# First stage of a language-model tower: each four gathers wait for the four issued three groups ago

## The reference

```
emb = word_emb[x] + pos_emb                        # 64 x 128 x 192
for each of 3 graphs: ev = word_emb[ids]           # 64 x 128 x 192
    g_j = relu(mean_over_rows(adj_j @ ev) @ W_j.T + b_j)     # 64 x 16
y  = concat([emb, g_1, g_2, g_3]) @ W_proj.T + b_proj
h  = layernorm(y) * gamma + beta                   # first stage up to here
h += long_convolution(layernorm(h)) + bias term    # filter from a small sine network
h += mixture_of_experts(layernorm(h))              # 8 experts, top 2, 192 -> 768 -> 192, gelu
```

## Time and profile before

| | us |
|---|---|
| median of 3 runs | 1004.51 (1003.2 to 1005.33) |
| profiled execution | 999.54 |
| its span | 997.7 |
| PE busy | 872.5 (87%) |
| DVE busy | 658.9 (66%) |
| POOL busy | 636.2 (64%) |
| ACT busy | 535.8 (54%) |

### The profile page before, as it was taken

How to read it: one execution, slowest core, us unless ns; L and a number is a source line. 1 busy time by engine, 2 the same in 40 slices (tenths; PEclk the granted TensorE clock), 3 DMA queues, 4 the chain that set the end, 5 groups by cost and what they waited for, 6 DMA issues and landing times.

```text
span 997.7 us, 22836 instructions
## 1 busy us (share of the span) xinstructions
PE 872.5 (87%) x7469; PEld 828.4 (83%) x7469; DVE 658.9 (66%) x2142; ACT 535.8 (54%) x1271; POOL 636.2 (64%) x552
## 2 busy tenths in 40 slices
PE   3969899898788839894779999999999999999993
PEld 2959899888788828893569999999999989999993
DVE  3167857777667664977846777677666666666662
ACT  1222232223222134579947777777777767777771
POOL 6777777777777500100057887588777768888886
PEclk9957556655665659997589999999999999999997
DMA  7427647457374339882956445835754554343454
GB/s 252 124 83 254 202 123 252 140 189 246 89 245 143 123 84 286 211 254 65 216 154 173 60 60 99 247 57 93 193 127 62 96 132 61 62 64 62 60 58 45
DMA packets 99788, 138.31 MB, mean 139 GB/s; under 512 B 13427, under 2 KB 81430, under 8 KB 97654
## 3 DMA queue, kind: packets, MB, share of 16 engines
q0 software_dynamic: 39552, 53.26, 27.8%
q1 hardware_dynamic: 59142, 73.59, 23.9%
q10 hardware_dynamic: 1008, 10.34, 2.8%
HBM read 98.14 MB, written 39.02 MB: 137 GB/s over the span
## 4 chain that ended last, share of the span: by engine, by line
POOL 26%; PE 26%; DMA 25%; issue 12%; DVE 6%; ACT 3%; DVEq 1%; POOLq 0%; SPq 0%
DMA out<-Hs,id_s 20%; POOL ev_g L520 16%; POOL emb_g L512 6%; POOL blob L536 3%; PE bank L798 3%; PE bank L800 3%; PE bank L799 3%; DMA emb_g<-in_word_emb,ids_i 2%; PE bank L779 2%; PE bank L780 2%; PE bank L782 2%; PE bank L781 2%; PE bank L783 2%; DVE hstats L1156 2%; DMA ev_g<-in_word_emb,ids_i 1%
## 5 line engine op out<-in xcount | busy, mean ns | idle before, releaser
L974 ACT ACTIVATE Hs<-bank,U 128x256 bf16<-128x256 f32 x426 | 214.1, 502 | 120.9 <-PE bank L783 120.9
L550 POOL DMA_INDIRECT out<-Hs,id_s x142 | 234.1, 1648 | 65.9 <-issue 46.8
L520 POOL DMA_INDIRECT ev_g<-in_word_emb,ids_i x192 | 188.3, 981 | 67.6 <-issue 56.4
L536 POOL DMA_INDIRECT blob<-xtab_d,id_g x142 | 144.9, 1020 | 122.6 <-DVEq L1339 79.7
L975 ACT ACTIVATE Hs<-bank,U 128x256 f32<-128x256 f32 x426 | 216.5, 508 | 0.0
L1361 DVE TENSOR_TENSOR Hs<-Hs 128x512 bf16<-128x512 f32 x213 | 147.2, 692 | 103.0 <-ACT Hs L975 102.6
L798 PE MATMUL bank<-U,Hs 128*128 128x192 bf16 x852 | 210.1, 247 | 0.3 <-issue 0.3
L800 PE MATMUL bank<-U,Hs 128*128 128x192 bf16 x852 | 208.8, 245 | 0.0
L799 PE MATMUL bank<-U,Hs 128*128 128x192 bf16 x852 | 208.5, 245 | 0.0
L779 PE MATMUL bank<-wst,U 128*128 128x256 bf16 x426 | 116.7, 274 | 1.3 <-DVE wst L1350 1.3
L780 PE MATMUL bank<-wst,U 128*128 128x256 bf16 x426 | 116.7, 274 | 0.0
(11 more groups left out here) (216 smaller groups left out, 1651.3 us busy)
## 6 DMA issues: line engine op xcount, KB each, us to landing
adj_s<-in_adj SPq DMA_DIRECT2D x48, 256.0 KB, 8.0
ev_g<-kpad_d SPq DMA_DIRECT2D x24, 512.0 KB, 5.8
U<-blob_d SPq DMA_DIRECT2D x14, 771.0 KB, 4.7
wst<-in_wsrc SPq DMA_DIRECT2D x8, 1344.0 KB
blob_d<-blob ACTq DMA_DIRECT2D x7, 1443.0 KB, 5.5
U<-blob_d SPq DMA_DIRECT2D x14, 672.0 KB, 5.5
xtab_d<-U SPq DMA_DIRECT2D x4, 1552.0 KB, 16.2
out<-Hs SPq DMA_DIRECT2D x4, 1536.0 KB, 12.8
```

The lines of the kernel that those rows point to most:

```text
L520: pool.indirect_dma_start(ev_g[:, p, j, b, :], None, t["word_emb"], bass.IndirectOffsetOnAxis(ap=ids_i[:, 1 + j, i * Q + b:i * Q + b + 1], ...
L536: pool.indirect_dma_start(xg_f[:, q % RX, h, :], None, xtab_d, bass.IndirectOffsetOnAxis(ap=id_g[:, 2 * q + h:2 * q + h + 1], axis=0)).the ...
L550: pool.indirect_dma_start(out, bass.IndirectOffsetOnAxis(ap=id_s[:, 2 * q + h:2 * q + h + 1], axis=0), yo[:, q % RY, h, :], None, compute_ ...
L974: f(hh[w][:, d, :], ps, ACT.Gelu, bias=bi[:, d:d + 1])
```

## The change

Every group of four gathers now waits for the landing of the group issued three groups before it. Before, E, v1 and v2 waited for the group two before them, and v0 had no landing wait. The waits on `emb_t` and `gvec` and the gathers themselves stay.

```diff
--- before.py
+++ after.py
@@ -506,16 +506,17 @@
             def gathers(i):
                 p = i % 2
                 if i > 0:
-                    pool.wait_ge(ev_in[1 - p][1], 16 * Q * ((i - 1) // 2 + 1))
+                    pool.wait_ge(ev_in[1 - p][0], 16 * Q * ((i - 1) // 2 + 1))
                 after(pool, emb_t, i - 1)
                 for b in range(Q):
                     pool.indirect_dma_start(emb_g[:, p, b, :], None, t["word_emb"],
                                             bass.IndirectOffsetOnAxis(ap=ids_i[:, 0, i * Q + b:i * Q + b + 1], axis=0)).then_inc(emb_in[p], 16)
                 after(pool, gvec, i - 1)
                 for j in range(GRAPHS):
-                    landed = emb_in[p] if j < 2 else ev_in[p][0]
-                    if j > 0:
-                        pool.wait_ge(landed, 16 * Q * (i // 2 + 1))
+                    if j == 2:
+                        pool.wait_ge(emb_in[p], 16 * Q * (i // 2 + 1))
+                    elif i > 0:
+                        pool.wait_ge(ev_in[1 - p][j + 1], 16 * Q * ((i - 1) // 2 + 1))
                     for b in range(Q):
                         pool.indirect_dma_start(ev_g[:, p, j, b, :], None, t["word_emb"],
                                                 bass.IndirectOffsetOnAxis(ap=ids_i[:, 1 + j, i * Q + b:i * Q + b + 1], axis=0)).then_inc(ev_in[p][j], 16)
```

## The result

| | before | after |
|---|---|---|
| median of the runs | 1005.33 us (5 runs, 1003.2 to 1008.03) | 997.75 us (5 runs, 995.12 to 998.45) |
| ratio, 95% interval | | 0.9926 (0.9898 to 0.9954) |
| profiled execution, its span | 999.54, 997.7 | 997.75, 995.9 |

The changed kernel is 7.6 us faster. A second comparison on another occasion gave 0.9901 (0.9873 to 0.9928), which is 9.9 us of 999.88; its medians, 988.43 against 999.88 us, lie 11.4 apart. So the change is worth 7 to 10 us by the two ratios, 5 to 13 by their intervals; 10.5 had been forecast.

A forecast was written before the change was run, and what follows sets the result against it. POOL's 11.4 us of pauses and PE's 11.2 us of gather waits were taken to bound the first stage side by side; 11.2 less 0.7 for delayed loads gives 10.5, so 1004.5 becomes 994.0 us, range 990.5 to 1001.

The forecast's parts named there:

- the added wait: On POOL, one more wait instruction per turn, condition already true: cost 0, at most 0.8 us.
- the buffers: POOL's wait for PE to have used buffers of two turns ago: 7.6 us left at turn 4, cost 0.
- PE held its pace: PE, turns 10 to 14: without gather waits they take 98.6 us, 19.72 a turn, as turns 6 to 9 did.
- The pauses: POOL, first stage: all seven waits for landings go, 11.4 us gained on POOL, bounds 0 and 11.4.
- the long gathers: POOL gathers that take longer while DVE splits an expert's weights; the change was said not to touch them.
- What then ends last: End of first stage: POOL's last landing 332.8, PE 333.1, so PE sets the end and the stage gains 11.2 us.
- The burst: Expert store, expert load and adjacency loads together: extra gathers delay direct loads, priced 0.7 us, up to 4.9.
- rival B: Late loads delay DVE's adjacency sums and PE waits at L602, halving the gain: 998.2 us; chance 0.19.
- C: POOL's deeper queue fills as well and it pauses one group later: no gain, 1004.5 us; chance 0.09.
- D: TensorE gets its lower clock more often without pauses: slower, 1011 us; chance 0.07 with any other loss.
- The spans: Whole profiled execution: span 997.7 less 10.5 gives 987.2 us; the same gain on the median gives 994.0.

The follow-up runs named there:

- the first pair: First profiles of the kernel before and the changed kernel; medians 1005.33 and 997.75 us, ratio 0.9926.
- the repetition: Kernel before and changed kernel each run once more, programs unchanged; 999.36 us (1.0007) and 988.43 us (0.9901 to before).
- short loads: Only 128 of 2688 columns loaded for experts 1 to 7, in the kernel before (995.40 us, 0.9924) and the changed kernel (992.73 us, 0.9918).

## Why the prediction was right, and where it was off

Right: the direction, the cause and the place. The seven pauses went, no new wait came in their place at POOL, landings stayed under 11.25 us, the added wait cost nothing that shows (gap 0.30 as before), the buffers stayed free (5.5 us at turn 4, the closest place, of the 7.6 before), PE held its pace (turns 10 to 14 took 98.9 us with no wait for a gather, 98.6 forecast), and what the stage gained came through to the experts' first fetch (7.9 and 9.7 us in the two pairs). 997.75 us lies in the range; the gain was 7.6 (9.9 on the second occasion), not 10.5. In the first pair the distance from 10.5 comes from two errors of the same sign, told next.

*The pauses*, priced at 11.4 us, are the mis-sized term. The waits view counts the whole idle time ahead of the gather, and 7 x 0.30 of it is the issue gap that stays. The removable part was 9.2 us (8.7 in the repetition).

*A term that was missing.* "The change does not touch those", said of the long gathers, holds for their cause and not for their length. Which gather meets DVE's subtraction or an adjacency sum, and where in it, shifts with POOL's pace: 251.6 to 256.6 us of gathers with the same passes on DVE. It took 2.3 us in the first pair and gave 0.4 in the second. The repetitions (251.6 and 254.4 for the same kernel) make this chance between executions rather than a price of the change.

*What then ends last.* "So PE sets the end by 0.3 us" was wrong, because POOL had been credited with too much: the last landing was forecast at 332.8 and came at 336.91, of which 2.2 us are the gaps counted as pauses and 2.3 the longer gathers, less 0.3 by a shorter landing. POOL's last landing still ends the stage: 3.13 us of waiting right ahead of PE's last matmuls where the forecast had under 2 in all, and 7.1 us in six waits in the repetition. The last gather, forecast at 329.8, came at 334.21 and 331.05. That PE is ready soon was right: it stood waiting from 333.82 (336.95 - 3.13), where 333.1 had been forecast.

*The burst*, priced at 0.7 us, and rival B (4.9): neither price shows. PE was ready 0.7 us later than forecast, but the last landing ended the stage, and short loads brought the changed kernel no gain. PE's waits for the adjacency sums rose from 2.5 to 5.3 us, which was named as the mark of B, but they were 3.8 in the repetition of before and 0.9 in that of after: a mark that varies by itself.

*C* falls with the pauses, *D* with the clock: 0.57 to 0.69 by turn, and not under 0.55. Turn 11, whose 0.67 the prediction had put down to its pause, has 0.69 without one. Turn 12 took 23.48 us at 0.57, but the kernel before has such a turn too (22.93 us at 0.57 in its repetition). That a burst delays the gathers was the cause of the pauses; that the gathers' depth delays the burst in return was not seen.

*The spans.* 987.2 had been forecast for the profiled span. The first profile has 995.9 and the repetition 983.5, so a single span misses by 8.7 us one way and 3.7 the other, whatever the change does. The medians, 997.75 and 988.43 beside a forecast of 994.0, lie 3.8 and 5.6 us off, each way once; what can be held against the forecast is the gain on one occasion, 7.6 and 9.9 us beside 10.5.

## What to carry to other kernels

Read a throttle on outstanding transfers in three numbers: the engine's time for one, the landing when nothing else runs, and the landing in a burst. Here 1.25, 2.7 and 7 to 8 us; a check has to look back further than the last of them (6.25 us did not, 11.25 did), and once it does, more depth brought nothing here but a longer median landing. When pricing a wait that goes away, subtract the gap that the engine has ahead of such an instruction anyway. And when a profiled span and the timed median disagree, compare by milestones, here the end of each stage, over at least two profiles of each kernel.

## What was not expected of the hardware

The experts' stage, whose program is the same in all these kernels, took 481.0 to 492.3 us in six profiles with the same data; what makes it vary was not looked for. The issue of one and the same indirect DMA took 0.94 to 2.48 us in the first stage. It was long, 1.19 us and more, only where it started inside one of DVE's passes over two inputs (fp32 less bf16 over 1536 elements a partition, or a sum of fp32 over 768 or 384), and then it ended 0.81 to 0.83 us behind that pass.
